# A state loop over two channel blocks at a time in a Mamba mixer on one core: order of the state pairs, loads of B and C, places of the gates

## Chip, cores and metric

One core of one Trainium2 chip. The metric is the device time of one execution in microseconds (us); the median of three runs of the kernel before is given below.

## What is computed

Two batches of 512 tokens with 512 channels go through three blocks: cross attention over 8192 context rows, a Mamba mixer with a feed-forward part, and a quantised feed-forward part with low-rank additions. The change touches the scan of the Mamba mixer, which in the reference is:

```python
deltaA = jnp.exp(delta[..., None] * A)
BX = (delta * xc)[..., None] * Bm[:, :, None, :]
def step(h, inp):
    dA, bx, c = inp
    h = dA * h + bx
    return (h, jnp.einsum('ben,bn->be', h, c))
y = jnp.swapaxes(ys, 0, 1) + D_param * xc
y = y * jax.nn.silu(z)
return y @ out_proj_w
```

There are 16 states for each of the 512 channels, and B and C (`Bm`, `Cm`) are one row of 512 tokens for each state, the same for all channels. After the mixer come a layer norm and a feed-forward part (`ffn_w1`, `ffn_w2`).

## The kernel before

The attention takes the span's first 2200 us or so and isn't touched. The state loop lies between 2334 and 2703 us, and much other work is laid beside it.

**Tiling.** 512 channels are four channel blocks e of 128 partitions (`KD` = 4). 16 states are eight state pairs q (`S_STEP` = 2, `S_PER` = 8). One step j of the loop is a pair of states of one channel block: `S_ALL` = 32 steps for a batch, `PAIRS` = 64 in all. A step is called pair j here. Before the change q is the outer loop and e the inner one: pairs 0 to 3 are q = 0 of the four blocks, and so on.

**What a pair does.** ScalarE computes the decays, two exponentials (L1796), into one of four slots of `dA`. VectorE's loop (L1338 to L1352) waits for them and runs two scans (L1344), then makes the inputs of the next pair (`inputs(j + 1)`, B times the step size, L1290), then multiplies the pair by C (L1350, it raises `s_hc`), then does what `beside(j)` puts there. TensorE adds the result to the block's sum in PSUM with two products by the identity (`y_sum`, L2141, it raises `s_ysum`) and then does its own `beside(j)` (L2189): projections, convolution and the step-size product of batch 1 during batch 0, and the feed-forward of batch 0 during batch 1. `inputs(j)` waits for the sum of pair j-4, since `bx` has four slots too. Each engine runs its list in order.

**Rows of B and C.** They are stored to `bc_rows` in device memory (`store_bc`, L775) and read back spread over all 128 partitions into one of two slots of `BC` (`load_bc`, L782), 512 KB for B and 512 KB for C, one state pair q for all four channel blocks. Load n waits until all pairs that used its slot have been multiplied. `inputs` waits for it at e = 0 (L1285). All of this is issued on SP's queue, in the order of the code (L804 to L820): batch 0's eight loads, with `out_proj` behind the fourth; `store_bc(1)`, which waits for its own completion; a wait until the last step-size product of batch 1 is done (`unit_ready(sp, (1, "dt", KD - 1))`, L814; TensorE does these products beside pair 24, `DT_1`); four pieces of the feed-forward's weights, 1 MB each (`load_piece`, L801); then batch 1's eight loads, from the fifth on each with another piece behind it.

**Gates.** Once a channel block's eight state pairs are summed, `gate(b, e)` (L1250) adds D times x and multiplies by the gate: two VectorE instructions, L1256 and L1258. With q outside, no block is complete before the last four pairs of its batch: `GATE_0` puts batch 0's gates beside pairs 31 (three) and 32 (one), `GATE_1` batch 1's first two beside pairs 62 and 63; the other two follow the loop (L1474). `mix` (L2089) on TensorE, the output projection, waits for all four; batch 0's stands beside pairs 32 and 33. The step sizes of batch 1 (`step_sizes`, L1241) stand beside pairs 30 to 33, and the norm behind the mixer of batch 0 beside pairs 33 to 35, followed by the feed-forward from pair 36 on.

Of the kernel before, what the change touches and what calls it, by code (L numbers as in the profile page):

```python
# [17 lines left out]
NTOK = 512  # L18
# [193 lines left out]
S_PER = NS // S_STEP  # L212
S_ALL = KD * S_PER
PAIRS = NB * S_ALL
EXP_LEAD = 3


# [7 lines left out]
Z_1 = (DBC_1 - 1, DBC_1 + 1, DBC_1 + 2, DBC_1 + 3)  # L225
DT_1 = DBC_1 + 4
DELTA_1 = S_ALL - 2
GATE_0 = {S_ALL - 1: (0, 1, 2), S_ALL: (3,)}
GATE_1 = PAIRS - 2
MIX_0 = S_ALL  # L230
LN2_0 = MIX_0 + 1
TURN_2 = LN2_0 + NT // 2
# [8 lines left out]
PIECE = 4  # L241
PIECES_1 = F2 // P // PIECE
PER_BATCH = 2 * PIECES_1


def stage(b, name):
# [36 lines left out]
def emit(nc, t_in, out):  # L283
    with ExitStack() as ctx:
# [340 lines left out]
        def _(sp):  # L625
# [153 lines left out]
                             ).then_inc(s_bcst, 16)  # L779
                sp.wait_ge(s_bcst, b * 16 + 16)  # L780

            def load_bc(b, q):  # L782

                n, size = b * S_PER + q, S_STEP * NTOK
                if n >= 2:
                    sp.wait_ge(s_hc, KD * (n - 1))
                for a in range(2):
                    sp.dma_start(BC[:, n % 2, a, :, :].rearrange("p s n -> p (s n)"),
                                 bc_rows[b, a, q * size:(q + 1) * size].partition_broadcast(P)
                                 ).then_inc(s_bc[n % 2], 16)  # L790
# [11 lines left out]
                             src.rearrange("(k p) n -> p k n", p=P)).then_inc(s_ring[n % RING], 16)  # L802

            store_bc(0)  # L804
            for q in range(2):
                load_bc(0, q)
            for q in range(2, S_PER):
                load_bc(0, q)
                if q == 3:
                    unit_ready(sp, (1, "xw2", NT - 1))  # L810
                    sp.dma_start(w_out[:], t_in["out_proj"].rearrange("(k p) n -> p k n", p=P)
                                 ).then_inc(s_w["outp"], 16)
            store_bc(1)
            unit_ready(sp, (1, "dt", KD - 1))  # L814
            for n in range(RING):
                load_piece(n)
            for q in range(S_PER):
                load_bc(1, q)
                if q >= 4:
                    load_piece(q)  # L820

            def load_integers(i, dst, parts):

# [124 lines left out]
        def _(dve):  # L948
# [301 lines left out]
            def gate(b, e):  # L1250

                w = (b, "ssm", e)
                dve.wait_ge(s_ysum, b * S_ALL + S_ALL - KD + (e + 1))
                if e == 0:
                    unit_emptied(dve, (b, "xz", 2 * KD - 1))
                empties(dve.scalar_tensor_tensor(xc[b][:, e, :], xc[b][:, e, :], col("Dp", e), bank(w),  # L1256
                                                 ALU.mult, ALU.add), w)
                dve.tensor_tensor(zs[b][:, e, :], zs[b][:, e, :], xc[b][:, e, :], ALU.mult).then_inc(s_y, 1)  # L1258
# [19 lines left out]

            def inputs(j):

                b, i = divmod(j, S_ALL)
                q, e = divmod(i, KD)
                n = b * S_PER + q
                if e == 0:
                    dve.wait_ge(s_bc[n % 2], 32 * (n // 2 + 1))  # L1285
                if q == 0:
                    dve.wait_ge(s_delta, b * KD + (e + 1))
                if j >= S_SLOTS:
                    dve.wait_ge(s_ysum, j - S_SLOTS + 1)
                dve.tensor_tensor(bx[:, j % S_SLOTS, :, :], BC[:, n % 2, 0, :, :],  # L1290
                                  dx[b][:, e, :].unsqueeze(1).broadcast_to([P, S_STEP, NTOK]),
                                  ALU.mult).then_inc(s_bx, 1)

            def beside(j):

                for k in range(NT + 1):
                    if j == NORM_1[k]:
                        half_norm(1, 2 * k)
                        half_norm(1, 2 * k + 1)
                if j == TURN_1:  # L1300
                    add_norm(1)
                for e in GATE_0.get(j, ()):
                    gate(0, e)
                if DELTA_1 <= j < DELTA_1 + KD:
                    step_sizes(1, j - DELTA_1)
                if j == LN2_0:
                    mixed(0, 0)
                    mixed(0, 1)
                if j == LN2_0 + 1:
                    mixed(0, 2)  # L1310
                    second_norm(0, 0)
                    mixed(0, 3)
                    second_norm(0, 1)
                if j == LN2_0 + 2:
                    second_norm(0, 2)
                    second_norm(0, 3)
                if GATE_1 <= j:
                    gate(1, j - GATE_1)

            attended(1)  # L1320
# [16 lines left out]
            inputs(0)  # L1337
            for j in range(PAIRS):  # L1338
                slot = j % S_SLOTS
                n = j // KD  # L1340
                dve.wait_ge(s_dA, j + 1)
                dve.wait_ge(s_bx, j + 1)
                for s in range(S_STEP):
# [171 lines left out]
        def _(act):  # L1515
# [269 lines left out]
            decays(0)  # L1785
            logs(0)
            for j in range(PAIRS):
                b, i = divmod(j, S_ALL)
                q, e = divmod(i, KD)
                if q == 0:  # L1790
                    act.wait_ge(s_delta, b * KD + (e + 1))
                if j >= S_SLOTS:
# [41 lines left out]
        def _(pe):  # L1834
# [296 lines left out]

            def y_sum(j):

                b, i = divmod(j, S_ALL)
                q, e = divmod(i, KD)
                w = (b, "ssm", e)
                if q == 0:
                    unit_free(pe, w)
                pe.wait_ge(s_hc, j + 1)
                for s in range(S_STEP):  # L2140
                    last = pe.matmul(bank(w), ident[:], bx[:, j % S_SLOTS, s, :], start=(q == 0 and s == 0),  # L2141
                                     stop=(q == S_PER - 1 and s == S_STEP - 1))
                last.then_inc(s_ysum, 1)
# [165 lines left out]
```

## Time and profile before

| | us |
|---|---|
| median of 3 runs (2994.95 to 2996.25) | 2995.61 |
| the profiled execution's own time | 2997.04 |
| its span, first to last instruction | 2995.2 |
| TensorE, matmuls, busy | 2904.2 |
| VectorE busy | 2205.6 |
| ScalarE busy | 1671.3 |
| GpSimd busy | 2044.9 |
| DMA moved | 296.26 MB |

The granted clock of TensorE is 0.983 of full speed in the mean. Busy time is the time in which an instruction of the engine runs; since the stages have different limits, a share of the span says little about one stage. A timeline row gives the start, the duration, the engine, the line, the operation with output and inputs, the shapes and the number of instructions, and in brackets the idle time ahead of it with what ended it. `SPq` is SP issuing a DMA: the duration is that of issuing, not of the transfer. "To landing" is the time from the issue to completion.

### The profile page before, as it was taken

The page shows a single profiled execution, that of the slowest core. Times are in us where ns is not written, and L with a number is a line of the kernel's source. Part 1 is how long each engine was busy: PE and PEld are TensorE (multiplying, and loading weights), DVE is VectorE, ACT ScalarE, POOL GpSimd, SP SyncE. Part 2 cuts the span into 40 slices and gives each one's busy share as a digit, 9 for nine tenths or more (in the row PEclk, how much of TensorE's full clock was granted, in tenths as well). Part 3 has the DMA queues.
Part 4 walks back from the last instruction along what each step waited for, and adds up shares of the span by engine and source line. Part 5 has one row for each costly group of instructions (what it writes and reads, how often), then busy time and mean ns, then how long its engine had stood idle before and what let it go on. Part 6 is the DMA issues. An engine that isn't in the chain of part 4 may idle for free.

```text
span 2995.2 us, 41476 instructions
## 1 busy us (share of the span) xinstructions
PE 2904.2 (97%) x14776; PEld 1827.8 (61%) x14776; DVE 2205.6 (74%) x3296; ACT 1671.3 (56%) x2956; POOL 2044.9 (68%) x761
## 2 busy tenths in 40 slices
PE   7999999999999999999999999999999887899999
PEld 4666666666666666666666666666544333445587
DVE  7777777777777777777777777777646999987653
ACT  1467676666667666666666666666631565422021
POOL 1599999999999999999999999999930000002000
PEclk9999999999999999999999999999989998999999
DMA  5544454444435455443544444444250112215100
GB/s 163 133 99 109 98 117 101 97 110 103 114 90 119 101 121 139 111 110 86 117 101 108 100 109 111 92 113 102 69 184 27 41 47 99 85 56 170 70 15 18
DMA packets 145760, 296.26 MB, mean 99 GB/s; under 512 B 36050, under 2 KB 41170, under 8 KB 135986
## 3 DMA queue, kind: packets, MB, share of 16 engines
q1 hardware_dynamic: 135908, 226.76, 27.6%
q0 software_dynamic: 9072, 66.06, 11.8%
q8 instruction: 120, 1.97, 0.3%
q10 hardware_dynamic: 576, 0.79, 0.1%
q14 instruction: 84, 0.69, 0.1%
HBM read 114.47 MB, written 8.06 MB: 41 GB/s over the span
## 4 chain that ended last, share of the span: by engine, by line
PE 90%; DVE 6%; ACT 1%; SPq 1%; issue 1%; POOL 0%; DMA 0%; DVEq 0%; POOLq 0%; ACTq 0%
PE ps L1905 17%; PE ps L1931 16%; PE ps L1944 15%; PE ps L1857 9%; PE ps L1881 9%; PE ps L1888 9%; PE ps L2161 4%; PE ps L2125 3%; PE ps L2141 3%; PE ps L1961 2%; PE ps L1913 1%; DVE bx L1344 1%; SPq L671 1%; DVE pm L1082 1%; PE ps L2153 1%
## 5 line engine op out<-in xcount | busy, mean ns | idle before, releaser
L1082 DVE TENSOR_REDUCE pm<-ps 128x1 f32<-128x512 f32 x2048 | 1403.3, 691 | 539.3 <-PE ps L1905 457.6
L1579 ACT ACTIVATE pf<-ps 128x512 f32<-128x512 f32 x2048 | 1203.5, 603 | 655.0 <-PE ps L1931 572.0
L925 POOL TENSOR_TENSOR psum<-psum,pf 128x2048 f32<-128x2048 f32 x317 | 1456.0, 4593 | 18.7
L1905 PE MATMUL ps<-ks,qs 96*128 96x512 f32 x2048 | 833.4, 407 | 10.3 <-DMA qs<-QL 3.6
L1931 PE MATMUL ps<-qs,ks 98*128 98x512 f32 x2048 | 814.8, 399 | 1.6 <-ACT pf L1579 1.6
L1905 PEld LDWEIGHTS ps<-ks,qs 96*128 96x128 f32 x2048 | 386.9, 189 | 197.9 <-issue 109.5
L1944 PE MATMUL ps<-pf,V 128*32 128x512 f32 x4096 | 472.5, 602 | 0.0
L1931 PEld LDWEIGHTS ps<-qs,ks 98*128 98x128 f32 x2048 | 391.4, 191 | 46.3 <-ACT pf L1579 12.5
L940 POOL TENSOR_TENSOR ring_r<-ring,w_hi 128x512 fp32r<-128x512 f32 x16 | 21.8, 1374 | 550.8 <-ACT w_hi L1812 550.8
L925 POOL TENSOR_TENSOR psum<-pf 128x2048 f32<-128x2048 f32 x64 | 308.9, 4827 | 51.2 <-ACT pf L1579 51.2
L1881 PE MATMUL ps<-cTh,Wkg 128*128 128x512 f32 x732 | 301.0, 411 | 0.2 <-POOL cTl L889 0.2
L1944 PEld LDWEIGHTS ps<-pf,V 128*32 128x32 f32 x4096 | 121.0, 111 | 266.7 <-issue 234.2
L1888 PE MATMUL ps<-Wvh,cTh 128*128 128x256 f32 x768 | 219.2, 285 | 0.7 <-DVE KL L1067 0.7
L1888 PE MATMUL ps<-Wvh,cTl 128*128 128x256 f32 x768 | 219.4, 286 | 0.0
L1888 PE MATMUL ps<-Wvl,cTh 128*128 128x256 f32 x768 | 218.9, 285 | 0.0
L2141 PE MATMUL ps<-bx,ident 128*128 128x512 f32 x256 | 135.5, 658 | 45.6 <-DVE bx L1350 45.6
L1881 PEld LDWEIGHTS ps<-cTh,Wkg 128*128 128x128 f32 x732 | 138.9, 190 | 57.0 <-ACT V L1565 32.8
L1888 PEld LDWEIGHTS ps<-Wvh,cTh 128*128 128x128 f32 x768 | 147.1, 192 | 30.2 <-issue 1.2
L1888 PEld LDWEIGHTS ps<-Wvl,cTh 128*128 128x128 f32 x768 | 146.9, 191 | 29.0 <-issue 1.5
L1888 PEld LDWEIGHTS ps<-Wvh,cTl 128*128 128x128 f32 x768 | 146.7, 191 | 22.3 <-issue 1.0
L1344 DVE TENSOR_TENSOR_SCAN bx<-dA,bx 128x512 f32<-128x512 f32 x128 | 149.3, 1208 | 3.3 <-ACT dA L1796 3.1
L1881 PE MATMUL ps<-cTl,Wkg 128*128 128x512 f32 x366 | 149.8, 409 | 0.0
(237 smaller groups left out, 3045.3 us busy)
## 6 DMA issues: line engine op xcount, KB each, us to landing
ks<-KH SPq DMA_DIRECT2D x1024, 64.0 KB, 2.0
psum<-pf POOLq DMA_DIRECT2D x63, 1024.0 KB, 8.8
ks<-KL SPq DMA_DIRECT2D x512, 64.0 KB, 2.0
cT<-in_ctxT SPq DMA_DIRECT2D x32, 768.0 KB, 6.9
Wkg<-wk_rows SPq DMA_DIRECT2D x61, 384.0 KB, 3.1
BC<-bc_rows SPq DMA_DIRECT2D x32, 512.0 KB, 4.8
ring<-in_ffn_w SPq DMA_DIRECT2D x16, 1024.0 KB, 8.0
wA<-in_W_fcT SPq DMA_DIRECT2D x4, 1024.0 KB, 11.5
```

The source lines that it names most:

```text
L925: pool.tensor_tensor(acc, before, pf[:, tile % P_SLOTS, :], ALU.add).then_inc(s_sum, 1)
L1082: dve.tensor_reduce(pm[:, of % 2, n // BLK, n % BLK:n % BLK + 1], src, AX.X, ALU.max).then_inc(s_wfree, 1)
L1344: last = dve.tensor_tensor_scan(bx[:, slot, s, :], dA[:, slot, s, :], bx[:, slot, s, :], 0.0, ALU.mult, ALU.add)
L1579: act.activation(pf[:, tile % P_SLOTS, j * NTOK:(j + 1) * NTOK], ps[:, S_BANK + u % S_BANKS, :], ACT.Exp, scale=SCALE).then_inc(s_exp, 1)
L1857: last = pe.matmul(bank(w)[0:m, 0:rhs.free_size()], lhsT, rhs, start=(i == 0), stop=(i == len(pairs) - 1))
L1881: last = pe.matmul(dst, w[term == 2], (cTh, cTl)[term == 1][:, f, half], start=(n == 0), stop=(n == TERMS - 1))
L1888: last = pe.matmul(dst[:, m * 2 * P:(m + 1) * 2 * P], (cTh, cTl)[term == 2][:, f, t * P:(t + 1) * P], (Wvh, Wvl)[term == 1][:, f, pair], s ...
L1905: last = pe.matmul(dst, qs[0:3 * HD, h, t * P:(t + 1) * P], ks[0:3 * HD, keys_of(of, j), i * 512:(i + 1) * 512], start=True, stop=True)
L1931: pe.matmul(ps[:, S_BANK + u % S_BANKS, :], ks[0:SROWS, keys_of(g, j), m * P:(m + 1) * P], qs[0:SROWS, h, :], start=True, stop=True).then_ ...
L1944: last = pe.matmul(ps[j * HD:(j + 1) * HD, O_BANK, :], V[:, g // 2 % 2, m, at:at + HD], pf[:, tile % P_SLOTS, j * NTOK:(j + 1) * NTOK], st ...
L2141: last = pe.matmul(bank(w), ident[:], bx[:, j % S_SLOTS, s, :], start=(q == 0 and s == 0), stop=(q == S_PER - 1 and s == S_STEP - 1))
L2161: pe.matmul(bank(x), lhsT, rhs, start=(i == 0), stop=False)
```

## The change

The loop over state pairs takes two channel blocks at a time (`EH` = 2) through all eight state pairs, then the other two: pairs 0 to 15 of a batch are blocks 0 and 1, pairs 16 to 31 blocks 2 and 3. `state_pair(j)` gives batch, q and e, `last_pair(b, e)` a block's last pair. A load of B and C serves two pairs instead of four, so each state pair's rows are fetched twice in a batch: 32 loads n in all, load n for pairs 2n and 2n + 1. On SP 14 loads stand ahead of `store_bc(1)`, with `out_proj` behind load 7; loads 14 and 15 of batch 0 stand with batch 1's, behind the four pieces. Pieces 4 to 7 go behind loads 23, 25, 27 and 29. Batch 0's first two gates go beside pairs 16 and 17, the other two stay beside 31 and 32; batch 1's first two go beside pairs 48 and 49.

```diff
--- before.py
+++ after.py
@@ -212,6 +212,7 @@
 S_PER = NS // S_STEP
 S_ALL = KD * S_PER
 PAIRS = NB * S_ALL
+EH = 2
 EXP_LEAD = 3
 
 
@@ -225,8 +226,8 @@
 Z_1 = (DBC_1 - 1, DBC_1 + 1, DBC_1 + 2, DBC_1 + 3)
 DT_1 = DBC_1 + 4
 DELTA_1 = S_ALL - 2
-GATE_0 = {S_ALL - 1: (0, 1, 2), S_ALL: (3,)}
-GATE_1 = PAIRS - 2
+GATE_0 = {S_ALL // 2: (0,), S_ALL // 2 + 1: (1,), S_ALL - 1: (2,), S_ALL: (3,)}
+GATE_1 = S_ALL + S_ALL // 2
 MIX_0 = S_ALL
 LN2_0 = MIX_0 + 1
 TURN_2 = LN2_0 + NT // 2
@@ -241,6 +242,19 @@
 PIECE = 4
 PIECES_1 = F2 // P // PIECE
 PER_BATCH = 2 * PIECES_1
+
+
+def state_pair(j):
+
+    b, i = divmod(j, S_ALL)
+    half, i = divmod(i, EH * S_PER)
+    q, e = divmod(i, EH)
+    return b, q, half * EH + e
+
+
+def last_pair(b, e):
+
+    return b * S_ALL + (e // EH + 1) * EH * S_PER - EH + e % EH
 
 
 def stage(b, name):
@@ -779,11 +793,12 @@
                              ).then_inc(s_bcst, 16)
                 sp.wait_ge(s_bcst, b * 16 + 16)
 
-            def load_bc(b, q):
-
-                n, size = b * S_PER + q, S_STEP * NTOK
+            def load_bc(n):
+
+                b, q, _ = state_pair(EH * n)
+                size = S_STEP * NTOK
                 if n >= 2:
-                    sp.wait_ge(s_hc, KD * (n - 1))
+                    sp.wait_ge(s_hc, EH * (n - 1))
                 for a in range(2):
                     sp.dma_start(BC[:, n % 2, a, :, :].rearrange("p s n -> p (s n)"),
                                  bc_rows[b, a, q * size:(q + 1) * size].partition_broadcast(P)
@@ -802,11 +817,9 @@
                              src.rearrange("(k p) n -> p k n", p=P)).then_inc(s_ring[n % RING], 16)
 
             store_bc(0)
-            for q in range(2):
-                load_bc(0, q)
-            for q in range(2, S_PER):
-                load_bc(0, q)
-                if q == 3:
+            for n in range(S_ALL // EH - 2):
+                load_bc(n)
+                if n == 7:
                     unit_ready(sp, (1, "xw2", NT - 1))
                     sp.dma_start(w_out[:], t_in["out_proj"].rearrange("(k p) n -> p k n", p=P)
                                  ).then_inc(s_w["outp"], 16)
@@ -814,10 +827,10 @@
             unit_ready(sp, (1, "dt", KD - 1))
             for n in range(RING):
                 load_piece(n)
-            for q in range(S_PER):
-                load_bc(1, q)
-                if q >= 4:
-                    load_piece(q)
+            for n in range(S_ALL // EH - 2, PAIRS // EH):
+                load_bc(n)
+                if S_ALL // EH + RING + 3 <= n < PAIRS // EH - 1 and n % 2 == 1:
+                    load_piece(RING + (n - S_ALL // EH - RING - 3) // 2)
 
             def load_integers(i, dst, parts):
 
@@ -1250,7 +1263,7 @@
             def gate(b, e):
 
                 w = (b, "ssm", e)
-                dve.wait_ge(s_ysum, b * S_ALL + S_ALL - KD + (e + 1))
+                dve.wait_ge(s_ysum, last_pair(b, e) + 1)
                 if e == 0:
                     unit_emptied(dve, (b, "xz", 2 * KD - 1))
                 empties(dve.scalar_tensor_tensor(xc[b][:, e, :], xc[b][:, e, :], col("Dp", e), bank(w),
@@ -1278,10 +1291,9 @@
 
             def inputs(j):
 
-                b, i = divmod(j, S_ALL)
-                q, e = divmod(i, KD)
-                n = b * S_PER + q
-                if e == 0:
+                b, q, e = state_pair(j)
+                n = j // EH
+                if j % EH == 0:
                     dve.wait_ge(s_bc[n % 2], 32 * (n // 2 + 1))
                 if q == 0:
                     dve.wait_ge(s_delta, b * KD + (e + 1))
@@ -1314,7 +1326,7 @@
                 if j == LN2_0 + 2:
                     second_norm(0, 2)
                     second_norm(0, 3)
-                if GATE_1 <= j:
+                if GATE_1 <= j < GATE_1 + EH:
                     gate(1, j - GATE_1)
 
             attended(1)
@@ -1337,7 +1349,7 @@
             inputs(0)
             for j in range(PAIRS):
                 slot = j % S_SLOTS
-                n = j // KD
+                n = j // EH
                 dve.wait_ge(s_dA, j + 1)
                 dve.wait_ge(s_bx, j + 1)
                 for s in range(S_STEP):
@@ -1785,8 +1797,7 @@
             decays(0)
             logs(0)
             for j in range(PAIRS):
-                b, i = divmod(j, S_ALL)
-                q, e = divmod(i, KD)
+                b, q, e = state_pair(j)
                 if q == 0:
                     act.wait_ge(s_delta, b * KD + (e + 1))
                 if j >= S_SLOTS:
@@ -2131,8 +2142,7 @@
 
             def y_sum(j):
 
-                b, i = divmod(j, S_ALL)
-                q, e = divmod(i, KD)
+                b, q, e = state_pair(j)
                 w = (b, "ssm", e)
                 if q == 0:
                     unit_free(pe, w)
```

## Rows read from the trace of the kernel before

**Rows 1.** The page, busy time of each engine, share of the span, instructions.

```profile
PE 2904.2 (97%) x14776; PEld 1827.8 (61%) x14776; DVE 2205.6 (74%) x3296; ACT 1671.3 (56%) x2956; POOL 2044.9 (68%) x761
```

**Rows 2.** Windows: us, PE, PEld, DVE, ACT, POOL busy, PEclk, DMA share, GB/s.

```profile
2420.00:2497.00 77.00, 76.79 (x178) 33.49 (x179) 76.69 (x69) 52.18 (x69) 0.00 (x0) 1.00 0.20 68
2497.00:2561.00 64.00, 41.40 (x87) 17.12 (x85) 59.68 (x78) 33.88 (x57) 0.00 (x0) 0.76 0.28 100
2561.00:2703.00 142.00, 141.59 (x326) 62.64 (x327) 122.32 (x110) 41.15 (x66) 0.00 (x0) 0.99 0.20 67
```

**Rows 3.** VectorE's timeline, a bare pair (15) and the next scan.

```profile
2433.58 2.33 DVE L1344 TENSOR_TENSOR_SCAN bx<-dA,bx 128x512 f32<-128x512 f32 x2
2435.83 1.20 DVE L1290 TENSOR_TENSOR bx<-BC,dx 128x1024 f32<-128x1024 f32 x1
2436.95 1.22 DVE L1350 TENSOR_TENSOR bx<-bx,BC 128x1024 f32<-128x1024 f32 x1
2438.08 2.33 DVE L1344 TENSOR_TENSOR_SCAN bx<-dA,bx 128x512 f32<-128x512 f32 x2
```

**Rows 4.** Timelines near pair 48: TensorE's y_sum 46 and 47, VectorE's scan 49.

```profile
2612.99 1.88 PE L2141 MATMUL ps<-bx,ident 128*128 128x512 f32 x4
...
2618.14 1.88 PE L2141 MATMUL ps<-bx,ident 128*128 128x512 f32 x4
...
2612.04 2.33 DVE L1344 TENSOR_TENSOR_SCAN bx<-dA,bx 128x512 f32<-128x512 f32 x2
```

**Rows 5.** Tile BC from 2438 to 2440: issues of a quiet load, time to landing.

```profile
L788 SPq DMA_DIRECT2D BC<-bc_rows x2: 319/376/433, 2438.2 to 2438.6; - x2
...
DMA to landing us min/median/max: 3.7/4.2/4.8
```

**Rows 6.** Tile BC, loads at 2389 (out_proj behind) and 2587 (a piece behind).

```profile
DMA to landing us min/median/max: 3.6/4.8/5.9
...
DMA to landing us min/median/max: 3.8/4.6/5.5
```

**Rows 7.** SP's own timeline from 2475.2 to 2496.

```profile
2492.86 2.34 SPq L801 DMA_DIRECT2D ring<-in_ffn_w  x4
2495.25 2.06 SPq L788 DMA_DIRECT2D BC<-bc_rows  x1
```

**Rows 8.** Tile BC from 2492 to 2500: the load behind the four pieces.

```profile
L788 SPq DMA_DIRECT2D BC<-bc_rows x2: 595/1328/2060, 2495.2 to 2497.4; - x2
...
DMA to landing us min/median/max: 11.3/11.7/12.1
```

**Rows 9.** VectorE's timeline, scans 27, 29, 30, 31 and 32, two gates.

```profile
2487.59 2.33 DVE L1344 TENSOR_TENSOR_SCAN bx<-dA,bx 128x512 f32<-128x512 f32 x2
...
2494.73 1.22 DVE L1290 TENSOR_TENSOR bx<-BC,dx 128x1024 f32<-128x1024 f32 x1 [0.30 <-PE ps L2141]
...
2498.65 2.34 DVE L1344 TENSOR_TENSOR_SCAN bx<-dA,bx 128x512 f32<-128x512 f32 x2 [1.56 <-ACT dA L1796]
...
2504.80 2.34 DVE L1344 TENSOR_TENSOR_SCAN bx<-dA,bx 128x512 f32<-128x512 f32 x2 [1.56 <-ACT dA L1796]
...
2510.64 2.33 DVE L1344 TENSOR_TENSOR_SCAN bx<-dA,bx 128x512 f32<-128x512 f32 x2
...
2515.14 0.74 DVE L1256 SCALAR_TENSOR_TENSOR xc<-xc,cols,ps 128x512 f32<-128x512 f32 x1
...
2516.52 0.74 DVE L1256 SCALAR_TENSOR_TENSOR xc<-xc,cols,ps 128x512 f32<-128x512 f32 x1
...
2520.62 2.33 DVE L1344 TENSOR_TENSOR_SCAN bx<-dA,bx 128x512 f32<-128x512 f32 x2
```

**Rows 10.** TensorE's timeline, y_sum 24 and the dt products of batch 1.

```profile
2487.27 1.88 PE L2141 MATMUL ps<-bx,ident 128*128 128x512 f32 x4
2489.08 3.70 PE L1857 MATMUL ps<-dbc,w_dt 64*128 64x512 f32 x8
```

**Rows 11.** The page's DMA issues: a piece, KB, median us to landing.

```profile
ring<-in_ffn_w SPq DMA_DIRECT2D x16, 1024.0 KB, 8.0
```

## The prediction

> **What bounds the kernel now.** I read the page first: TensorE is busy for 97% of the span [rows 1]. That is a mean over stages, so I cut the state loop (2334 to 2703 us) with the windows view [rows 2]. From 2420 to 2497 TensorE is busy 76.8 of 77 us, from 2561 to 2703 141.6 of 142; from 2497 to 2561 it is busy only 41.4 of 64, while VectorE is busy 59.7. So between 2497 and 2561 VectorE sets the pace, and a delay of it there goes straight to the end, since behind 2561 TensorE works without a gap and has nothing to give back.
>
> Then the timeline of VectorE. The first scan of the loop is pair 0; counting on, the scan at 2433.58 is pair 15, that at 2438.08 pair 16, that at 2487.59 pair 27. A bare pair takes 4.50 us, scan to scan [rows 3]; the inputs of the next pair start 2.25 us behind the scan and 2.25 us ahead of the next one. TensorE takes 5.15 us for a pair with the product laid beside it (2612.99 to 2618.14, [rows 4]), so it falls behind by 0.65 us a pair up to pair 28, at most four pairs, the depth of the state slots. Last, the loads: what matters is when the rows of B and C have landed against when `inputs` wants them [rows 5 to 8].
>
> **The order of the pairs.** The same 64 scans, products and decays run, at the same durations; nothing is removed there. ScalarE's decays wait for a batch's third and fourth step sizes later than before; I give that nothing either way, since the waits for it that VectorE has at pairs 29 and 30, 1.56 us each [rows 9], vanish in the stall below anyhow.
>
> **Twice the loads.** 32 pairs of transfers instead of 16, each of 2 x 512 KB, now one for each two state pairs. Transfer n is issued when the multiplication of pair 2n-3 ends and is wanted by `inputs(2n)`. In a bare stretch: the multiplication of pair 15 starts at 2436.95 and ends 1.22 later, 2438.17; two scans on, the inputs of pair 18 would start at 2438.08 + 4.50 + 2.25 = 2444.8. That leaves 6.65 us [rows 3]. The load issued at 2438.2 to 2438.6 landed at most 4.8 us behind its issue [rows 5], so within 5.2. With a large transfer issued right behind it the second half needed 5.9 and 5.5 us [rows 6], 6.3 and 5.9 with the issue of the first. All are under 6.65, so I take no cost in quiet stretches, nor at load 7, which has `out_proj` behind it (cover left: 0.35 us), nor at loads 23 to 29, where TensorE's pace gives VectorE 5.15 us a pair. If this cover went, see the third rival.
>
> **The load of pairs 28 and 29.** This is the term that decides. Before, all rows of batch 0 are asked for ahead of `store_bc(1)`. Now the loop ahead of it ends at load 13, and load 14 stands on SP behind the store, behind the wait for the last `dt` product of batch 1, and behind four pieces of `ffn_w1`, 1 MB each. TensorE does that product at 2489.08 to 2492.8 [rows 10]; SP issues the pieces at 2492.86 and a load of B and C at 2495.25 [rows 7]. In the kernel before, that load is the first of batch 1, wanted only by pair 32. It landed 12.1 and 11.3 us after issue; the second half was issued at 2497.4 [rows 8], so all was there at 2497.4 + 11.3 = 2508.7. In the changed kernel load 14 stands in this very place of the queue; nothing ahead of it has moved, since TensorE reaches the product at the same time.
>
> It is wanted at `inputs(28)`, 2.25 us behind scan 27: 2487.59 + 2.25 = 2489.84 before [rows 9], and 2.8 us later now, because two gates have moved ahead of it: 2492.6. So VectorE stands still for 16.1 us. Queued behind the waiting instruction are the multiplication of pair 27, scan 28 and all else of VectorE; TensorE waits with `y_sum(27)`, SP with load 15.
>
> From there on, starting at 2508.7: 2.25 to scan 28, two bare pairs 9.00 (their decays were ready long before), pair 30 with its step sizes 5.84 (2504.80 to 2510.64), pair 31 9.98 less two gates. A gate costs 1.38 (2515.14 to 2516.52), so 9.98 - 2.76 = 7.22. Scan 32 starts at 2508.7 + 24.3 = 2533.0; before, at 2520.62 [rows 9]. **+12.4 us**. Load 15 is issued at 2508.7 + 2.3 = 2511.0, lands within 5.2, at 2516.2, and is wanted at 2508.7 + 2.25 + 4.50 + 2.25 = 2517.7: no second stall.
>
> Both ends of this term: if load 14 passed the pieces and landed in 5.2 us, as in [rows 5], it would be there at 2500.4 and scan 32 comes 8.3 us earlier, +4.1. If both halves took 12.1 us from 2497.4 on, and somewhat more, +14. I take the row of the same place in the queue.
>
> The page DMA: Bandwidth & Descriptors of the Trainium skill (Anatomy of one DMA) gives 2.0 us plus bytes by 436 GB/s for a transfer, fitted on another issuing path. For the 5.24 MB from 2492.86 on this is an estimate of 14.0 us, landing at 2506.9, and the change would cost 10.6 instead of 12.4 us. The trace says 2508.7 for the same bytes, and the sum goes by the trace.
>
> **The gates.** Gates 0 and 1 of batch 0 go from pair 31 to pairs 16 and 17. At pair 24 TensorE's `y_sum` starts at 2487.27 [rows 10], 8.6 us behind VectorE (pair 24 starts 3 x 4.50 ahead of pair 27 and takes 4.6 to the end of its multiplication: 2478.7); at pair 16 it was 8 x 0.65 less behind, 3.4 us, and the gates need sums from two pairs back: no wait. The 2 x 1.38 us come out of that lead, which TensorE covers, and what is left goes into the stall. At pair 31 they are saved, as counted. By itself this part would gain 2.8 us: added ahead of pair 28, it is absorbed by VectorE's 0.30, 1.56 and 1.56 us of waits [rows 9].
>
> In batch 1 gates 0 and 1 go to pairs 48 and 49. Gate 0 needs `y_sum(46)`, which ends at 2612.99 + 1.88 = 2614.9, while VectorE is there at 2612.04 [rows 4]: 2.8 us of a new wait, and 2 x 1.4 of work. Pair 50 then ends at 2614.9 + 1.4 + 4.6 + 1.4 + 4.6 = 2626.9, and TensorE, at 5.15 us a pair, wants it at 2612.99 + 4 x 5.15 = 2633.6. Cover 6.7 us, cost nothing; with the cover gone it would be 5.6. The last two gates stay where the 2703 us end is set by TensorE; saving two earlier ones there gives nothing.
>
> **TensorE's clock** stands at 1.2 GHz for part of the stretch 2497 to 2561 already (mean grant 0.76 in it [rows 2]). The stall lengthens the pause ahead of it. At 1.2 GHz a pair's sum takes twice the 1.88 us of [rows 4], 3.8, under VectorE's 4.5, so it follows all the same; only if the clock were to rise later, beside `mix`, would it cost, and I keep 3 us of the upper range for that.
>
> **Sum.** 0 + 0 + 12.4 + 0. Against the profiled execution's own 2997.0 us it makes 3009.4; the median of the runs is 1.4 lower, 2995.6, which gives 3008.0.
>
> **Rivals.**
> 1. *Load 14 overtakes the pieces* (they do not share an order). For it: a load's two halves might be served beside the larger transfers rather than behind them. Against it: the 12.1 and 11.3 us of the same load in the same place [rows 8], beside 4.8 in quiet. It gives +4.1, 2999.7. The same page of the Trainium skill (Queues, rings and completion order) states that one issuing engine's descriptors are taken in ring order, against this rival; rows 8 agree. Chance 0.09.
> 2. *Not slower: load 14 is in time, and the gates' 2.8 us at pair 31 remain.* One mechanism: SP gets past the `dt` product before VectorE comes to pair 28. Load 14 would have to land by 2492.6; the change turns into a gain if it lands ahead of 2508.7 - 12.4 = 2496.3. For that TensorE would have to finish the product over 5 us earlier, and it is busy without a gap from 2420 [rows 2]. It gives 2992.8. Chance 0.04.
> 3. *Loads late in quiet stretches too.* Twice the transfers; if a load took as long as a 1 MB transfer of its own, 8.0 us [rows 11] and 0.4 of issue, in place of 5.2, 1.75 would lack for each two pairs, of which TensorE's slower pace covers 1.3. Over loads 7 to 13 that is some 3 us, which delays the product and so load 14, and 1.75 more at load 15: 3013. Against it: no load in the trace that is not behind the pieces needs more than 6.3. Chance 0.09.
>
> The forecast keeps 0.78. Its own range is 3006 to 3010. The range given reaches past it towards the first and the third, 3003.5 to 3012.5. A measurement of this kernel tells about 0.2%, 6 us, from no change. Slower by more than that: the forecast and the third, 0.87. Within it: the first, and a little of the forecast's lower tail, 0.09. Faster: 0.04 is the second.
>
> **What would show it.** A single idle time of VectorE of about 16 us before the inputs of pair 28, released by the transfer of BC; four pieces issued on SP directly ahead of that load; landing about 12 us behind issue; three gates fewer than before at pair 31, leaving one; the run of TensorE without a gap starting near 2573 instead of 2561; no idle time of VectorE for a BC transfer elsewhere. I am wrong if that wait is under 10 us, if others on BC add up to more than 2 us, or if TensorE pauses behind pairs 48 to 50.

## The result, and the profile after

The kernel after takes 3005.03 us (median of 8 runs, 2998.15 to 3006.88); the kernel before, on the same chip, 2995.28 us (8 runs, 2991.06 to 2996.98). The ratio is 1.003, with a 95% interval of 1.0021 to 1.004: slower by some 9.8 us. The profiled execution took 3006.28 us with a span of 3004.1 us, against 2997.04 and 2995.2 before.

The page of the kernel after, busy time of the engines and the issues of the loads of B and C:

```profile
PE 2901.3 (97%) x14776; PEld 1826.3 (61%) x14776; DVE 2204.1 (73%) x3296; ACT 1669.0 (56%) x2956; POOL 2044.3 (68%) x761
...
BC<-bc_rows SPq DMA_DIRECT2D x64, 512.0 KB, 4.8
```

No engine does more than in [rows 1]; the instruction counts are the same. The loads are 64 halves now and land 4.8 us behind their issue in the median. So busy time explains nothing. The windows of the kernel after do (us, then busy us with instructions of PE, PEld, DVE, ACT and POOL, granted clock, DMA share, GB/s). They are the second and third stretch of [rows 2], with the bounds set where the same work now lies:

```profile
2495.00:2572.00 77.00, 43.85 (x88) 18.02 (x88) 63.41 (x79) 33.86 (x58) 0.00 (x0) 0.76 0.36 126
2572.00:2712.00 140.00, 139.49 (x325) 61.86 (x326) 120.82 (x110) 41.21 (x66) 0.00 (x0) 1.00 0.36 120
```

The middle stretch, in which TensorE is not full, was 64 us long and is 77 us now, with one matmul instruction more in it (88 against 87). The gapless run behind it begins near 2572 instead of 2561. Then VectorE's timeline of the kernel after (start, duration, engine, line, operation, shapes, count, in brackets the idle time ahead and what ended it); L1356, L1302 and L1362 are the scan, the inputs and the multiplication, L1269 is a gate's first instruction:

```profile
2440.81 0.75 DVE L1269 SCALAR_TENSOR_TENSOR xc<-xc,cols,ps 128x512 f32<-128x512 f32 x1
...
2446.70 0.74 DVE L1269 SCALAR_TENSOR_TENSOR xc<-xc,cols,ps 128x512 f32<-128x512 f32 x1
...
2488.60 2.33 DVE L1356 TENSOR_TENSOR_SCAN bx<-dA,bx 128x512 f32<-128x512 f32 x2
2506.94 1.22 DVE L1302 TENSOR_TENSOR bx<-BC,dx 128x1024 f32<-128x1024 f32 x1 [16.00 <-DMA BC<-bc_rows]
...
2524.05 2.33 DVE L1356 TENSOR_TENSOR_SCAN bx<-dA,bx 128x512 f32<-128x512 f32 x2
...
2528.55 0.74 DVE L1269 SCALAR_TENSOR_TENSOR xc<-xc,cols,ps 128x512 f32<-128x512 f32 x1
...
2531.27 2.33 DVE L1356 TENSOR_TENSOR_SCAN bx<-dA,bx 128x512 f32<-128x512 f32 x2
```

The scan at 2488.60 is pair 27. The inputs of pair 28 wait 16.00 us for the transfer of B and C. Scans 31 and 32 (2524.05 and 2531.27) are 7.22 us apart instead of 9.98 [rows 9], with one gate between them instead of three; the other two gates stand at 2440.81 and 2446.70 without a wait.

SP's timeline of the kernel after (the duration is that of issuing):

```profile
2491.10 2.33 SPq L816 DMA_DIRECT2D ring<-in_ffn_w  x4
```

TensorE's timeline of the kernel after:

```profile
2487.32 3.70 PE L1868 MATMUL ps<-dbc,w_dt 64*128 64x512 f32 x8
2490.94 3.70 PE L2151 MATMUL ps<-bx,ident 128*128 128x512 f32 x8
2509.35 3.61 PE L2151 MATMUL ps<-bx,ident 128*128 128x512 f32 x4 [14.71 <-DVE bx L1362]
...
2572.51 3.70 PE L1868 MATMUL ps<-tT,ring 128*128 128x512 f32 x8 [2.42 <-ACT tT L1668]
2576.05 1.88 PE L2151 MATMUL ps<-bx,ident 128*128 128x512 f32 x4
```

And the tile BC of the kernel after in the window 2491 to 2500, which holds load 14 alone:

```profile
L803 SPq DMA_DIRECT2D BC<-bc_rows x2: 532/1197/1862, 2493.5 to 2495.4; - x2
...
DMA to landing us min/median/max: 11.5/11.9/12.2
```

TensorE ends the `dt` product at 2491.0, SP issues the four pieces at 2491.10 and load 14 behind them, and its second half lands at 2495.4 + 11.5 = 2506.9, when VectorE goes on. The last of the four pieces, issued at 2492.6, landed 11.8 us later, at 2504.4, and the first half of load 14 at 2493.5 + 12.2 = 2505.7, so the landings came in the order of the issues. TensorE's own wait of 14.71 us follows from VectorE's.

**Where the time went.** In this execution the state loop began earlier: the first scan starts at 2333.17 instead of 2334.94, and the `dt` product at 2487.32, not at 2489.08 [rows 10]. These 1.76 us arise ahead of everything that the change touches. I therefore read positions against the start of that product:

| against the start of the `dt` product, us | before | after | difference |
|---|---|---|---|
| scan 32 | 31.54 | 43.95 | +12.41 |
| `y_sum(37)` on TensorE, where its gapless run has begun | 77.56 | 88.73 | +11.17 |

Behind that point the kernel after took 0.5 us less. 11.17 - 1.76 - 0.5 = 8.9, the difference of the spans.

### The profile page after: what moved, and what is told of

It reads as the page before. It is cut to its first block, busy times and chain, and to the rows that moved or that the text cites. A ratio compares the mean times of both kernels' runs of the same rounds, so it can differ in the third digit from the quotient of the medians.

```text
span 3004.1 us, 41525 instructions
## 1 busy us (share of the span) xinstructions
PE 2901.3 (97%) x14776; PEld 1826.3 (61%) x14776; DVE 2204.1 (73%) x3296; ACT 1669.0 (56%) x2956; POOL 2044.3 (68%) x761
## 3 DMA queue, kind: packets, MB, share of 16 engines
q0 software_dynamic: 9072, 66.06, 11.8%
## 4 chain that ended last, share of the span: by engine, by line
PE 89%; DVE 6%; SPq 1%; POOL 1%; issue 1%; ACT 1%; DMA 1%; DVEq 0%; POOLq 0%; ACTq 0%
PE ps L1916 17%; PE ps L1942 16%; PE ps L1955 15%; PE ps L1868 9%; PE ps L1892 9%; PE ps L1899 9%; PE ps L2171 4%; PE ps L2136 3%; PE ps L2151 3%; PE ps L1972 2%; DVE bx L1356 1%; PE ps L1924 1%; SPq L685 1%; POOL psum L938 1%; DVE pm L1095 1%
## 5 line engine op out<-in xcount | busy, mean ns | idle before, releaser
L1942 PEld LDWEIGHTS ps<-qs,ks 98*128 98x128 f32 x2048 | 391.8, 191 | 46.5 <-ACT pf L1591 12.4
L1356 DVE TENSOR_TENSOR_SCAN bx<-dA,bx 128x512 f32<-128x512 f32 x128 | 149.4, 1209 | 0.1
```

Source lines behind the costliest of these rows:

```text
L1356: last = dve.tensor_tensor_scan(bx[:, slot, s, :], dA[:, slot, s, :], bx[:, slot, s, :], 0.0, ALU.mult, ALU.add)
L1942: pe.matmul(ps[:, S_BANK + u % S_BANKS, :], ks[0:SROWS, keys_of(g, j), m * P:(m + 1) * P], qs[0:SROWS, h, :], start=True, stop=True).then_ ...
```

## The experiments

All are edits of the kernel after. "Against the product" is the position of `y_sum(37)` behind the `dt` product's start, less that of before. It leaves out what lies ahead of the loop, and is a check on the medians from one execution each. The kernel before was run again beside each group of experiments, and its medians differ (2993.65, 2992.45, 2992.96).

One thing lies in all these positions. The first product of the feed-forward stands directly ahead of `y_sum(37)`, and it took 5.40 us in the profile of the kernel before but 3.70 in that of the kernel after and in those of all experiments but the eighth, since the granted clock there differs (see the part on the prediction). So each of these positions, the kernel after's +11.17 among them, is 1.7 us lower than it was at that product's start, except for the eighth experiment's. Whether an edit decides which clock the product meets is open. Positions of the experiments other than the eighth can be compared with each other and with the kernel after free of it.

### All loads of batch 0 ahead of the store

```diff
-            for n in range(S_ALL // EH - 2):
+            for n in range(S_ALL // EH):
                 load_bc(n)
...
-            for n in range(S_ALL // EH - 2, PAIRS // EH):
+            for n in range(S_ALL // EH, PAIRS // EH):
```

> All 16 loads of batch 0 stand ahead of the store and the four pieces again; else as the changed kernel. Theory (place on the issuing queue, transfers served in order): the 16 us wait ahead of pair 28 is gone, but now load 16, which pair 32 wants, is the first behind the pieces. The store is issued near 2496 and completes near 2500, the pieces follow until 2503, and all 5.24 MB are down some 14 us after the first, near 2515 to 2516, where pair 32 wants them at 2513: a wait of 2 to 4 us there, against 2.8 gained by the gates. Time against the kernel before: -1 to +1 us. Rival (small loads pass the pieces): load 16 lands within 6 us of its issue, no wait, -2.8 us. Rival (twice the loads cost by themselves, wherever they stand): still +9 or more.

Measured: 2993.90 against 2993.65 us, ratio 0.9999 (0.999 to 1.0007); against the product +0.24. VectorE's timeline of this kernel, and then SP's:

```profile
2513.40 1.22 DVE L1302 TENSOR_TENSOR bx<-BC,dx 128x1024 f32<-128x1024 f32 x1 [3.23 <-DMA BC<-bc_rows]
```

```profile
2493.00 0.43 SPq L792 DMA_DIRECT2D bc_rows<-dbc  x1
2497.60 2.29 SPq L816 DMA_DIRECT2D ring<-in_ffn_w  x4
```

The whole loss is gone with two loads moved by a few lines. What remains is a wait of 3.23 us ahead of pair 32, about what the gates moved from pair 31 save (2.8 us): load 15 now holds the store up to 2493.00, the store the pieces up to 2497.60, and load 16 comes behind these.

### The first load of batch 1 ahead of the pieces as well

```diff
             store_bc(1)
+            load_bc(S_ALL // EH)
             unit_ready(sp, (1, "dt", KD - 1))
             for n in range(RING):
                 load_piece(n)
-            for n in range(S_ALL // EH - 2, PAIRS // EH):
+            for n in range(S_ALL // EH + 1, PAIRS // EH):
```

together with the edit above.

> As e1, but load 16 (batch 1's first) too stands ahead of the pieces, behind the store. Theory: no wait of VectorE for a transfer of BC anywhere; what is left of the change is the two gates gone from pair 31, 2 x 1.38 us, so -2.8 us against the kernel before, some -12.4 against the changed one. Rival (twice the loads cost by themselves): slower than before, and waits for BC in quiet stretches. Rival (gates at 16 and 17 and at 48 and 49 cost as much as they save): 0 against the kernel before.

Measured: 2990.42 against 2993.65 us, ratio 0.9987 (0.9979 to 0.9996); against the product -3.40. The tile BC over the whole run:

```profile
L803 SPq DMA_DIRECT2D BC<-bc_rows x64: 319/432/517, 2310.4 to 2662.3; - x64
...
  PE ps L2152: 3.1, 7
...
DMA to landing us min/median/max: 3.5/4.7/7.9
```

In the same view the kernel after has issues of up to 1862 ns, landings of up to 12.2 us, and the wait:

```profile
L803 SPq DMA_DIRECT2D BC<-bc_rows x64: 319/432/1862, 2312.2 to 2678.6; - x64
...
  DMA BC<-bc_rows: 16.0, 1
...
DMA to landing us min/median/max: 3.4/4.8/12.2
```

With loads 14 to 16 ahead of the pieces there is no wait for B and C at all; load 17, now the first behind them, is wanted late enough. So 32 loads instead of 16 and the new order of the pairs cost nothing that shows. Scan 32 starts 28.77 us behind the product, against 31.54 before: 2.77 us, the two gates that moved. Not all of it arrives. `y_sum` 32 with the first two products of `mix` takes 1.1 us longer than before (11.23 us, from 2519.07 to 2530.30, against 10.10; from 2513 to 2521 the granted clock is 0.50), and the feed-forward's first product starts only 1.7 us earlier behind the `dt` product; the other 1.7 of the 3.40 are that product's own 3.70 instead of 5.40 us. By the medians the change with its loads placed so is worth some 3 us, and the place of three loads cost 13 (3.2 + 9.75; 14.6 by the positions).

### The gates back, the loads as in the kernel after

```diff
-GATE_0 = {S_ALL // 2: (0,), S_ALL // 2 + 1: (1,), S_ALL - 1: (2,), S_ALL: (3,)}
+GATE_0 = {S_ALL - 1: (0, 1, 2), S_ALL: (3,)}
```

> The changed kernel with batch 0's gates where they were, three beside pair 31 and one beside 32. Theory: VectorE comes to pair 28 two gates earlier, and waits 2.8 us longer for load 14, 18.8 instead of 16.0, until the same moment; then pair 31 takes 2.8 us more. So the changed kernel's time + 2.8, some +12.5 us against the kernel before (measured) or +15 by the sum. Rival (the gates are hidden by something else at pair 31): the changed kernel's time.

Measured: 3007.14 against 2993.65 us, ratio 1.0043 (1.0031 to 1.0055), 13.5 us over before where the kernel after is 9.75; against the product +14.09. VectorE:

```profile
2505.47 1.22 DVE L1302 TENSOR_TENSOR bx<-BC,dx 128x1024 f32<-128x1024 f32 x1 [18.71 <-DMA BC<-bc_rows]
...
2532.57 2.33 DVE L1356 TENSOR_TENSOR_SCAN bx<-dA,bx 128x512 f32<-128x512 f32 x2
```

The end of the wait is fixed by the load, and what VectorE has not done ahead of it lengthens the wait: 18.71 instead of 16.00, the 2.7 us of two gates, which then stand at pair 31 again. So the gates ahead of the stall are free and those saved behind it count in full, as the sum had it.

### Loads 14 and 15 ahead of the pieces, behind the wait for `dt`

```diff
             unit_ready(sp, (1, "dt", KD - 1))
+            for n in range(S_ALL // EH - 2, S_ALL // EH):
+                load_bc(n)
             for n in range(RING):
                 load_piece(n)
-            for n in range(S_ALL // EH - 2, PAIRS // EH):
+            for n in range(S_ALL // EH, PAIRS // EH):
```

> The changed kernel with loads 14 and 15 behind the wait for the dt product as before, but ahead of the four pieces. It splits the stall into SP's wait for the product and the pieces' transfer. Theory (pieces' bytes hold the load back): load 14 is issued right behind the product, lands 5.2 us later, the wait ahead of pair 28 is 5.5 to 6 us instead of 16, scan 32 comes some 10.5 us earlier than in the changed kernel: +1 to +3 us against the kernel before. Rival (most of the stall is SP's wait, not the pieces): wait still over 12 us, +8 or more.

Measured: 2998.14 against 2993.65 us, ratio 1.0013 (1.0005 to 1.0022); against the product +3.60. VectorE's timeline of this kernel, and then SP's:

```profile
2494.87 1.22 DVE L1304 TENSOR_TENSOR bx<-BC,dx 128x1024 f32<-128x1024 f32 x1 [5.18 <-DMA BC<-bc_rows]
...
2516.66 1.23 DVE L1304 TENSOR_TENSOR bx<-BC,dx 128x1024 f32<-128x1024 f32 x1 [2.35 <-DMA BC<-bc_rows]
```

```profile
2489.85 8.21 SPq L803 DMA_DIRECT2D BC<-bc_rows  x4
2498.11 3.71 SPq L816 DMA_DIRECT2D ring<-in_ffn_w  x4
```

This splits the 16.00 us. With the pieces behind it, load 14 costs 5.18 us of waiting: it is issued at 2489.85, when VectorE comes to want it, so this is nearly all the load's own transfer. The other 10.8 us are the 4 MB ahead of it. The time itself missed my expectation of +1 to +3: the pieces now start at 2498.11 and load 16 stands behind them, which gives a second wait of 2.35 us that I had not thought of. The pieces harm the load that follows them directly, here and in the first experiment.

### Batch 1's last two step sizes later

On top of the second experiment:

```diff
-DELTA_1 = S_ALL - 2
+DELTA_1 = {S_ALL - 2: 0, S_ALL - 1: 1, S_ALL + 6: 2, S_ALL + 7: 3}
...
-                if DELTA_1 <= j < DELTA_1 + KD:
-                    step_sizes(1, j - DELTA_1)
+                if j in DELTA_1:
+                    step_sizes(1, DELTA_1[j])
```

The new loop order allows it: blocks 2 and 3 are wanted only 16 pairs into the batch. It tests the prediction's reading that VectorE alone sets the pace from 2497 to 2561.

> e2's order of the loads, and the step sizes of blocks 2 and 3 of batch 1 moved from pairs 32 and 33 to 38 and 39: the new order of the pairs wants them only at pair 48. Theory (between 2497 and 2561 VectorE sets the end, behind it TensorE covers it): 2 x 1.34 us go off VectorE's list where it counts, and the end comes 2.7 us earlier than e2's, 5.5 to 6 us ahead of the kernel before. Rival (TensorE's clock or its wait for batch 0's mix takes the gain back, since DVE now reaches the mixer's result while TensorE is still at it): e2's time within 0.5 us.

Measured: 2990.24 against 2992.45 us, ratio 0.9991 (0.9982 to 1.0); against the product -3.33, where the second experiment had -3.40. No gain. VectorE, of this kernel and then of the second experiment's (L1278 takes over `mix`):

```profile
2527.43 0.69 DVE L1278 TENSOR_TENSOR xa<-xa,ps 128x512 f32<-128x512 f32 x1 [2.27 <-PE ps L1869]
...
2530.86 0.69 DVE L1278 TENSOR_TENSOR xa<-xa,ps 128x512 f32<-128x512 f32 x1 [1.61 <-PE ps L1869]
```

```profile
2530.50 0.69 DVE L1278 TENSOR_TENSOR xa<-xa,ps 128x512 f32<-128x512 f32 x1 [1.30 <-PE ps L1869]
```

The 2.7 us taken off VectorE come back as 2.6 us of waits for `mix` (2.27 + 1.61 - 1.30). At pairs 32 and 33 TensorE ends last, not VectorE; that reading of mine falls for this place.

### Batch 1's gates back at the end

On top of the second experiment:

```diff
-GATE_1 = S_ALL + S_ALL // 2
+GATE_1 = PAIRS - 2
```

> e2 with batch 1's first two gates back beside pairs 62 and 63. Theory (TensorE's lead of pairs covers the new 2.7 us wait and the 2.8 us of gates at pairs 48 and 49): e2's time, within 0.5 us. Rival (the wait at pair 48 reaches the end): up to 5.6 us faster than e2.

Measured: 2989.88 against 2992.45 us, ratio 0.999 (0.9982 to 0.9999); against the product -3.35 beside -3.40. In the kernel after, gate 0 of batch 1 does wait at pair 48:

```profile
2624.32 0.75 DVE L1269 SCALAR_TENSOR_TENSOR xc<-xc,cols,ps 128x512 f32<-128x512 f32 x1 [2.72 <-PE ps L2151]
```

and TensorE covers it: its sums of pairs 46 to 51 stay 5.15 us apart. A visible stall of 2.72 us that costs nothing.

### One channel block at a time

On top of the second experiment `EH = 1`, so that a load serves one pair only, with 28 loads ahead of the store and 5 more ahead of the pieces, `out_proj` behind load 15, the pieces 4 to 7 behind loads 45, 49, 53 and 57.

```diff
-EH = 2
+EH = 1
```

> One channel block at a time: rows of B and C fetched four times in a batch, one load for each pair, 28 loads ahead of the store. It takes the cover away on purpose. Theory (a load can only be issued when the pair two back has been multiplied, and takes 5.0 to 5.2 us to land): the cover falls from 6.65 us to 2.15, so every bare pair waits 2.9 to 3.1 us for its rows and takes 7.4 to 7.6 us instead of 4.5; the whole kernel some 130 to 180 us slower. Rival (transfers run at the DMA engines' rate, 1.05 MB in 2.7 us at 390 GB/s, and the rest of the time to landing is hidden): bare pairs take 4.5 to 5.2 us, under 40 us slower.

Measured: 3142.87 against 2992.45 us, ratio 1.0499 (1.048 to 1.0518). The tile BC, and VectorE's timeline:

```profile
L803 SPq DMA_DIRECT2D BC<-bc_rows x128: 319/428/508, 2311.9 to 2834.8; - x128
...
  DMA BC<-bc_rows: 167.4, 55
...
DMA to landing us min/median/max: 3.4/4.7/10.8
```

```profile
2551.28 2.33 DVE L1358 TENSOR_TENSOR_SCAN bx<-dA,bx 128x512 f32<-128x512 f32 x2
2556.58 1.23 DVE L1304 TENSOR_TENSOR bx<-BC,dx 128x1024 f32<-128x1024 f32 x1 [2.97 <-DMA BC<-bc_rows]
...
2558.86 2.33 DVE L1358 TENSOR_TENSOR_SCAN bx<-dA,bx 128x512 f32<-128x512 f32 x2
```

A load takes as long as in the kernel after (4.7 us in the median, against 4.8), but now one scan-to-scan pitch less, 4.50 us, lies between its issue and its need: the cover falls from 6.65 to 2.15 us. 5.2 less 2.15 is 3.05, the wait is 2.97, and a pair takes 7.58 us. Of the 64 pairs 55 wait, 167.4 us in all. This shows what the cover of 6.65 us in the kernel after is worth: with 6.65 the loads cost nothing, with 2.15 the whole difference to 5.2, in each of the pairs that wait.

### TensorE kept busy through the thin stretch

On top of the second experiment, 14 products whose result nobody reads, behind `y_sum` and `beside` of six pairs, into a bank that is free then:

```diff
+WARM = {27: 2, 28: 2, 29: 2, 30: 2, 31: 3, 34: 3}
...
+            def keep_clock(j):
+
+                if j in WARM:
+                    w = (0, "mix_out" if j < MIX_0 else "ln2_T", 0)
+                    pe.wait_ge(s_w["outp"], 16)
+                    unit_free(pe, w)
+                    for _ in range(WARM[j]):
+                        pe.matmul(bank(w), ident[:], w_out[:, 0, :], start=True, stop=True)
+
             for j in range(PAIRS):
                 y_sum(j)
                 beside(j)
+                keep_clock(j)
```

> e2, and TensorE multiplies by the identity into a free bank in its idle time beside pairs 27 to 31 and 34 (14 products that nobody reads), so that the clock should not fall. Theory (moving VectorE's step sizes gained nothing because TensorE, at 1.2 GHz in y_sum 32 and part of mix, is what ends last there): y_sum 32 and 35 take 1.9 us instead of 3.75, two products of mix 7.0 instead of 7.85, the turn 2.3 instead of 3.0; VectorE's 1.3 us wait for mix goes, and 2.4 us at pair 35: 3 to 4 us ahead of e2. Rival (TensorE's clock is hidden there): e2's time. Rival (the added products get in the way of the sums): slower than e2.

Measured: 2988.67 against 2992.96 us, ratio 0.9985 (0.9976 to 0.9994), 4.3 under before where the second experiment is 3.2 under its own; against the product -4.01. Windows of this kernel, then of the second experiment's, over the same 8 us (columns as above):

```profile
2513.00:2521.00 8.00, 5.25 (x13) 2.17 (x12) 7.93 (x10) 5.85 (x9) 0.00 (x0) 1.00 0.52 202
```

```profile
2513.00:2521.00 8.00, 4.48 (x6) 1.38 (x6) 7.90 (x11) 6.29 (x9) 0.00 (x0) 0.50 0.77 294
```

The granted clock stays at 1.00 of 2.4 GHz instead of 0.50, that is 1.2 GHz, with twice the products in the stretch. Here are TensorE's timelines, of this kernel (its `dt` product first) and of the second experiment's:

```profile
2483.66 3.70 PE L1870 MATMUL ps<-dbc,w_dt 64*128 64x512 f32 x8
...
2518.97 7.03 PE L1870 MATMUL ps<-w_out,zs 128*128 128x512 f32 x16
...
2551.97 5.40 PE L1870 MATMUL ps<-tT,ring 128*128 128x512 f32 x8 [2.65 <-ACT tT L1670]
```

```profile
2522.61 7.85 PE L1869 MATMUL ps<-w_out,zs 128*128 128x512 f32 x16
...
2556.19 3.70 PE L1869 MATMUL ps<-tT,ring 128*128 128x512 f32 x8 [2.13 <-ACT tT L1669]
```

`mix` is shorter by 0.8 us and the sum ahead of it by 1.8 (1.96 instead of 3.75), and the feed-forward's first product starts 2.3 us earlier against the `dt` product. But there the clock is low in this execution (0.68 granted from 2551.9 to 2557.2), so that the product takes 5.40 instead of 3.70 us and gives 1.7 us back. I expected 3 to 4 us over the second experiment; by the medians it is 1.1, by the position against the product 0.6, and the two intervals overlap. That the clock was held in this execution is shown; that this alone is a gain over the second experiment is not.

### Both

The same 14 products as in the experiment above, and the step sizes of blocks 2 and 3 later, as in the fifth.

> e8 with the step sizes of blocks 2 and 3 of batch 1 at pairs 38 and 39, as in e5. Theory: with mix at full clock most of VectorE's 2.7 us counts now, since its 3.9 us of waits for mix in e5 fall by the 2.7 us that y_sum 32 and mix gain: 1 to 2.5 us ahead of e8, some 8 us ahead of the kernel before. Rival (something else binds at pairs 32 and 33): e8's time.

Measured: 2985.66 against 2992.96 us, ratio 0.9971 (0.9959 to 0.9982), 7.3 us under before, 3.0 under the experiment above; against the product -5.68 after -4.01. The six runs of this kernel (2982.74 to 2986.58) lie under all eleven of that one (2987.42 to 2990.40), though the two intervals overlap slightly. VectorE waits for `mix` again, where it didn't in the experiment above, and TensorE's timeline shows why:

```profile
2524.64 0.69 DVE L1279 TENSOR_TENSOR xa<-xa,ps 128x512 f32<-128x512 f32 x1 [1.07 <-PE ps L1870]
...
2528.07 0.69 DVE L1279 TENSOR_TENSOR xa<-xa,ps 128x512 f32<-128x512 f32 x1 [1.61 <-PE ps L1870]
```

```profile
2484.32 3.70 PE L1870 MATMUL ps<-dbc,w_dt 64*128 64x512 f32 x8
...
2517.84 3.34 PE L2153 MATMUL ps<-bx,ident 128*128 128x512 f32 x4 [2.75 <-DVE bx L1364]
...
2552.66 3.70 PE L1870 MATMUL ps<-tT,ring 128*128 128x512 f32 x8 [2.18 <-ACT tT L1670]
```

The time taken off VectorE (2.7 us) comes back as waits for `mix` (1.07 + 1.61), as in the fifth experiment. The filler products did not hold the clock here: the sum ahead of `mix` takes 3.34 us where it took 1.96 (0.65 granted from 2516 to 2520). The feed-forward's first product starts 68.34 us behind the `dt` product, in the experiment above 68.31 (2551.97 - 2483.66), so the moved step sizes have gained nothing up to there. All of the 1.67 us between the two positions is the length of that product, 3.70 us at the full clock (1.00 granted from 2551 to 2557) instead of 5.40. My reading that work taken off VectorE would count once the clock was kept is not borne out by this execution. The 3.0 us between the medians are measured, but what makes them, beyond this product, is not shown. Against the kernel before this is the fastest of the versions measured.

## Why the prediction was right, and where it was off

**Right in the cause and nearly in size.** Forecast 3008.0, measured 3005.0 us; forecast difference 12.4 us, measured 9.75 by the medians, 11.2 at `y_sum(37)` against the product.

- *The load of pairs 28 and 29.* Predicted a wait of 16.1 us, with the pieces directly ahead of load 14 and a landing some 12 us behind issue; measured 16.00, and 12.2 and 11.5. Scan 32 was to come 12.4 us later and came 12.41 later against the product. That [rows 8] could be used for another load held because that load stood in the same place of the same queue. The first and the fourth experiment show the cause: moved ahead of the pieces alone, the load costs 5.18 us of waiting; ahead of the store, none.
- *Twice the loads cost nothing.* Shown by the second experiment, with no wait for B and C in 64 half loads, and from the other side by the one with one block at a time. The third rival is out: the kernel after has one wait for B and C in its whole loop, and its loads land 4.8 us behind their issue in the median. The first rival is out too: load 14 did not pass the pieces.
- *The second rival's gain exists* (2.77 us at scan 32, two gates), but only once the load is moved. For the kernel as changed its condition was not met: the load landed at 2506.9, not by 2496.3.
- *The gates.* Ahead of the stall free, behind it counted in full (third experiment); at pair 48 a wait of 2.72 where 2.8 was worked out, covered by TensorE (sixth).

Of the three signs of being wrong that the prediction names, none appeared.

**Off: what comes behind scan 32.** I let the 12.4 us go to the end undiminished, since "from 2497 to 2561 VectorE sets the pace", and kept 3 us upward for the clock. Two things there were off.

- The stretch is not VectorE's alone. At pairs 32 and 33 the sum and `mix` on TensorE end last, by the fifth experiment. In the kernel after, VectorE waits for `mix` 0.70 us where it was 0.18 before. This is the cost that the 3 us were kept for, the clock rising later beside `mix`: from the start of `y_sum` 32 to that of `y_sum` 33 TensorE takes 10.62 us (the sum 3.75, the first two products of `mix` 7.24) instead of 10.10 (3.40 and 7.03). It came to 0.5 us.
- No term of the sum was for the feed-forward's first product meeting the other level of the clock. It takes 3.70 us in the kernel after (1.00 granted from 2572.5 to 2576.0) and took 5.40 in the profile before (0.67 granted from 2561.4 to 2566.6). These are TensorE's rows of the kernel before, to be laid beside those of after at 2572.51:

```profile
2561.41 5.40 PE L1857 MATMUL ps<-tT,ring 128*128 128x512 f32 x8 [2.72 <-ACT tT L1656]
2566.64 1.88 PE L2141 MATMUL ps<-bx,ident 128*128 128x512 f32 x4
```

1.7 us come back there, 0.5 are lost at `mix`: 12.41 - 1.7 + 0.5 = 11.2, the +11.17 of the table. The rest, down to the 8.9 us between the two spans, is the 1.76 us ahead of the loop, which the change doesn't touch, and the 0.5 behind, whose cause isn't shown. At the start of the feed-forward's first product the difference is still 12.9 us (85.19 against 72.33 behind the `dt` product), close to the 12.4 forecast; whether the change makes this product run faster, or chance, no run decides. The medians' 9.75 us hold these effects and also what lies ahead of the loop, which differs by several us from one execution to the next: the first scan starts at 2334.94 us in the profile before, at 2333.17 in that of after, and at 2328.80 in the earliest of the experiments.

The Trainium skill's estimate (DMA: Bandwidth & Descriptors, Anatomy of one DMA), 14.0 us for the 5.24 MB by a formula fitted on another issuing path, stands against 15.8 us measured in the kernel after, from 2491.10 to 2506.9, the same as in the kernel before. The same page of the Trainium skill (Queues, rings and completion order) states that descriptors are consumed in ring order. This case agrees: the last piece landed at 2504.4, the two halves of load 14 behind it at 2505.7 and 2506.9.

**Open.** Whether the product at the feed-forward's start meets the low or the high clock: 5.40 us in the profiles of the kernel before and of the eighth experiment, 3.70 in that of the kernel after and in the other eight experiments, among them the ninth, whose filler products are those of the eighth. I did not find what decides it. One profile of each kernel can't tell either whether a kernel always meets the same level. Nor was a kernel of before tried with filler products, so what they are worth without the new loop order isn't known. Last, load 14 was moved along SP's queue only. From 2496 to 2504 the DMA engines moved 390 and 392 GB/s, so whether its order in the queue held it back, or 4 MB in flight would have done so from any queue, isn't shown: no run issued it on another engine.

## What to carry to other kernels

A transfer's time from issue to landing includes what its own queue holds ahead of it: here 4 MB ahead made 12 us of 4.8, so when loads are moved in an issuing engine's program, read what each one passes and what it waits behind, and give the one with the least slack the place ahead of the bulk transfers. A doubly buffered load is free while the work between its issue and its need is longer than its landing (6.65 against 5.2 us), and costs the whole difference at each turn where it is shorter (2.15: 3 us a pair, 150 us in all). Work taken off one engine counts only as far as the other engine is not the next to end last: 2.7 us off VectorE came back as 2.6 us of waits for TensorE. And a position taken behind a short product at the end of a thin stretch holds what clock that product met, here 1.7 us: compare ahead of it as well.

## What the runs showed that was not expected

- Issuing itself slows behind large transfers: the first half of load 14 held SP for 1862 ns, where the median is 432 and where, in the second experiment, 517 is the most. [rows 7] has the same with 2.06 us.
- A thin stretch at half clock can be lifted with products that nobody reads: 14 of them turned a granted 0.50 into 1.00 for 8 us in the eighth experiment. It isn't sure to hold: with the same 14 in the ninth, the sum of pair 32 ran for the most part at the low clock (3.34 us instead of 1.96).
- The loads of 512 KB land as fast with 128 of them (4.7 us in the median) as with 64 (4.8 in the kernel after, 4.7 in the second experiment); not their number costs, but the time left for each.
